# Key sums of the first attention from unsplit exponentials, and its values scaled one head later

## What is computed

```
scores = einsum('bhqd,bhkd->bhqk', q, k) / sqrt(128)
probs  = softmax(scores, axis=-1)
values = einsum('bhqk,bhkd->bhkd', probs, v)     # = v * probs.sum(over q)
out    = einsum('bsf,fh->bsh', values, w_o)
```

## Time and profile before

| | |
|---|---|
| median of 3 runs | 847.89 us |
| profiled execution | 848.14 us |
| its span, first to last instruction | 846.3 us |
| TensorE busy | 782.1 us, 92% |
| VectorE, ScalarE, GpSimd busy | 64%, 43%, 44% |
| granted TensorE clock, mean | 0.969 of 2.4 GHz |
| heads of the first attention | about 17 to 241 us |

### The profile page before, as it was taken

How to read it: one execution, slowest core, us unless ns; L and a number is a source line. 1 busy time by engine, 2 the same in 40 slices (tenths; PEclk the granted TensorE clock), 3 DMA queues, 4 the chain that set the end, 5 groups by cost and what they waited for, 6 DMA issues and landing times. The chain is left out here.

```text
span 846.3 us, 12715 instructions
## 1 busy us (share of the span) xinstructions
PE 782.1 (92%) x4092; PEld 599.9 (71%) x4092; DVE 538.5 (64%) x1049; ACT 359.8 (43%) x843; POOL 373.7 (44%) x339
## 2 busy tenths in 40 slices
PE   7899999999969889999999997988887896999997
PEld 5788888888844457888888885754445343788886
DVE  4666666677678964333333357799984698864535
ACT  3555555555541062232323234368884001543422
POOL 2221212123118924656565643799972885521100
PEclk9999999999989979999999999999999897999999
DMA  9210101010201014433333340000000012000001
GB/s 317 65 51 25 50 25 50 25 50 27 68 13 43 20 58 112 131 112 107 112 107 116 90 121 10 1 2 1 2 2 1 25 50 69 0 16 17 1 1 50
DMA packets 27054, 45.24 MB, mean 53 GB/s; under 512 B 3424, under 2 KB 16608, under 8 KB 26752
## 3 DMA queue, kind: packets, MB, share of 16 engines
q1 hardware_dynamic: 27008, 44.65, 17.7%
HBM read 43.45 MB, written 1.18 MB: 53 GB/s over the span
## 5 line engine op out<-in xcount | busy, mean ns | idle before, releaser
L1479 PE MATMUL bank<-xTh,ringh 128*128 128x512 f32 x420 | 169.5, 403 | 0.6 <-DVE xTl L1150 0.6
L1480 PE MATMUL bank<-xTl,ringh 128*128 128x512 f32 x420 | 166.2, 396 | 0.0
L1481 PE MATMUL bank<-xTh,ringl 128*128 128x512 f32 x420 | 166.0, 395 | 0.0
L1219 DVE TENSOR_TENSOR arena<-bank,arena 128x512 f32<-128x512 f32 x48 | 33.2, 691 | 114.9 <-ACT arena L881 105.7
L1481 PEld LDWEIGHTS bank<-xTh,ringl 128*128 128x128 f32 x420 | 79.3, 189 | 18.9
L1479 PEld LDWEIGHTS bank<-xTh,ringh 128*128 128x128 f32 x420 | 79.6, 190 | 16.7 <-issue 1.6
L1480 PEld LDWEIGHTS bank<-xTl,ringh 128*128 128x128 f32 x420 | 79.5, 189 | 15.1
L632 POOL TENSOR_TENSOR arena<-arena 128x512 f32<-128x512 f32 x48 | 62.6, 1303 | 51.6 <-DVE HTl L1223 49.5
L881 ACT ACTIVATE arena<-bank 128x512 f32<-128x512 f32 x48 | 28.7, 598 | 126.1 <-PE bank L1481 126.0
L555 POOL CAST ringh<-ring 128x768 fp32r<-128x768 f32 x15 | 12.7, 846 | 152.4 <-DMA ring<-w_attn 149.4
L1517 PE MATMUL bank<-outh,HTh 128*128 128x256 f32 x192 | 54.9, 286 | 3.1 <-DVE outl L1064 1.2
(11 more groups left out here) (269 smaller groups left out, 1971.7 us busy)
## 6 DMA issues: line engine op xcount, KB each, us to landing
ring<-w_moe SPq DMA_DIRECT2D x24, 256.0 KB, 2.9
arena<-route SPq DMA_DIRECT2D x16, 384.0 KB, 4.1
ring<-w_attn SPq DMA_DIRECT2D x15, 384.0 KB, 3.2
toep<-toep SPq DMA_DIRECT2D x32, 128.0 KB, 2.1
arena<-route SPq DMA_DIRECT2D x16, 256.0 KB, 4.1
outring<-w_down SPq DMA_DIRECT2D x24, 128.0 KB, 2.1
outring<-wo_attn SPq DMA_DIRECT2D x16, 128.0 KB, 2.0
arena<-route SPq DMA_DIRECT2D x16, 128.0 KB, 4.0
```

The costliest lines, as they stand in the source:

```text
L1219: dve.tensor_tensor(H1[:, i % LAG, :], bank[:, 1 + i % 2, :], SG[:, i % 2, :], ALU.mult).then_inc(gu_done, 1)
L1479: pe.matmul(o, ringh[:, slot, wc], xTh[:, k, halves[j]], start=(k == 0), stop=False)
L1480: pe.matmul(o, ringh[:, slot, wc], xTl[:, k, halves[j]], start=False, stop=False)
L1481: ins = pe.matmul(o, ringl[:, slot, wc], xTh[:, k, halves[j]], start=False, stop=(k == DK - 1))
```

## The change

For heads 0 to 14 the key sums are made another way. The exponentials E stay as they are, undivided and unsplit. VectorE writes the inverse row sums 32 times side by side (`inverse`), and TensorE multiplies, for each batch, these 32 columns (stationary) with E (moving, 128 columns) as one fp32 product into 32 rows of bank 2: eight products, the four batches of a half in four column groups (`sum_keys`). ScalarE copies the 256 columns out (`evac_key_sums`). SP writes one row of each group, 4 KB in all, to a buffer in DRAM, waits for it, and reads it back broadcast to all 128 rows (512 KB); it issues the next output weights and the next ring after that. `scale_v` then reads the sums from SBUF. Scaling and splitting of head h-1 move into head h on VectorE and ScalarE: on VectorE the two `scale_v` stand between the two row maxima and the two `low_v` behind the second, on ScalarE the two `high_v` stand between the two groups of exponentials, behind the copy of the first queries. TensorE's output product stays where it was; the key sums stand before chunks 2 to 5. Head 15 keeps the former way; its VectorE work and output weights come after the scaling and splitting of head 14. A semaphore that nothing used is dropped.

```diff
@@ -238,6 +238,10 @@
         VT = take(2 * TOK).rearrange("p (s t) -> p s t", s=2)
         VTc = take(TOK)
         E = take(TOK)
+        key_sums = take(2 * 2 * S).rearrange("p (s n) -> p s n", s=2)
+        spread_sums = take(2 * TOK).rearrange("p (s t) -> p s t", s=2)
+        inverse = take(B * 32).rearrange("p (b c) -> p b c", b=B)
+        sums_out = nc.dram_tensor("sums_out", (2, TOK), F32, kind="Internal").ap()
         outh = sb("outh", [P, 2, D], F32R)
         outl = sb("outl", [P, 2, D], F32R)
         nmax = sb("nmax", [P, B])
@@ -451,10 +457,26 @@
             load_x(1)
             sp.dma_start(outring[:, 0, :], wo_attn0[0, :, :]).then_inc(outring_in[0], 16)
 
+            def spread_key_sums(h, slot):
+                sp.wait_ge(ks_evac, h + 1)
+                settle(sp, sp_settled)
+                if not isinstance(h, int) or h >= 2:
+                    sp.wait_ge(sums_moved[slot], 16 * (h - slot))
+                    settle(sp, sp_settled)
+                    sp.wait_ge(vc_done, 2 * (h - 1))
+                    settle(sp, sp_settled)
+                sp.dma_start(sums_out[slot, :].rearrange("(j g s) -> g j s", j=2, g=4),
+                             key_sums[::32, slot, :].rearrange("g (j s) -> g j s", j=2)).then_inc(sums_moved[slot], 16)
+                sp.wait_ge(sums_moved[slot], 16 * (h - slot) + 16)
+                settle(sp, sp_settled)
+                sp.dma_start(spread_sums[:, slot, :], sums_out[slot, :].partition_broadcast(P)).then_inc(sums_moved[slot], 16)
+
             def load_attn0(h, slot):
                 sp.wait_ge(w_split, count(h - 1))
                 settle(sp, sp_settled)
                 sp.dma_start(ring[:, slot, 0:A_WO], w_attn0[h, :, :]).then_inc(ring_in[slot], 16)
+                if not isinstance(h, int) or h >= 2:
+                    spread_key_sums(h - 2, slot)
                 sp.wait_ge(wo_split, count(h - 1))
                 settle(sp, sp_settled)
                 sp.dma_start(outring[:, slot, :], wo_attn0[h, :, :]).then_inc(outring_in[slot], 16)
@@ -472,7 +494,9 @@
                 for w in range(2):
                     sp.dma_start(lowB[RANK * e:RANK * (e + 1), :, w, :], rows[w, e, :, :, :]).then_inc(lowb_in, 16)
             sp.dma_start(bias_bc[:], bias1.partition_broadcast(P)).then_inc(bias1_in, 16)
-            with sp.Fori(1, NH // 2) as i:
+            load_attn0(2, 0)
+            load_attn0(3, 1)
+            with sp.Fori(2, NH // 2) as i:
                 load_attn0(2 * i, 0)
                 load_attn0(2 * i + 1, 1)
 
@@ -506,6 +530,7 @@
 
             for h in range(4):
                 load_toep(toep0, 0, h, h)
+            spread_key_sums(NH - 2, 0)
             for n in range(2):
                 load_moe(n)
                 load_down(n)
@@ -785,15 +810,14 @@
 
             def exps(h, j):
                 act.wait_ge(nmax_done, 2 * h + j + 1)
-                act.wait_ge(el_done, count(2 * (h - 1) + j + 1))
+                act.wait_ge(ks_done, count(h))
                 for b in range(4 * j, 4 * j + 4):
                     ins = act.activation(E[:, b * S:(b + 1) * S], bank[:, 2 + j, (b % 4) * S:(b % 4 + 1) * S], ACT.Exp,
                                          bias=nmax[:, b:b + 1], scale=DH ** -0.5, accum_out=rowsum[:, b:b + 1])
                 ins.then_inc(exp_done, 1)
 
             def high_e(h, j):
-                act.wait_ge(en_done, 2 * h + j + 1)
-                act.wait_ge(csum_done, count(2 * (h - 1) + j + 1))
+                act.wait_ge(en_done, j + 1)
                 half = slice(j * HALF, (j + 1) * HALF)
                 act.activation(Eh[:, half], E[:, half], ACT.Copy).then_inc(eh_done, 1)
 
@@ -809,25 +833,33 @@
                 act.wait_ge(used, at)
                 act.activation(outh[:, slot, :], outring[:, slot, :], ACT.Copy).then_inc(wo_hi, 1)
 
+            def evac_key_sums(h, slot):
+                act.wait_ge(ks_done, h + 1)
+                if not isinstance(h, int) or h >= 2:
+                    act.wait_ge(sums_moved[slot], 16 * (h - slot))
+                act.activation(key_sums[:, slot, :], bank[:, 2, 0:2 * S], ACT.Copy).then_inc(ks_evac, 1)
+
             def head(h, slot):
                 last = isinstance(h, int) and h == NH - 1
+                exps(h, 0)
                 if not last:
                     evac_q(h + 1, 1 - slot, 0)
-                else:
+                if not isinstance(h, int) or h > 0:
+                    high_v(h - 1, 0)
+                    high_v(h - 1, 1)
+                exps(h, 1)
+                if last:
                     high_out(h, slot, out0_done, count(h - 1))
-                exps(h, 0)
-                if not last:
-                    evac_q(h + 1, 1 - slot, 1)
-                exps(h, 1)
-                high_e(h, 0)
-                high_e(h, 1)
-                if not last:
-                    high_out(h, slot, out0_done, count(h - 1))
-                high_v(h, 0)
-                high_v(h, 1)
-                if not last:
-                    evac_v(h + 1, 1 - slot, 0)
-                    evac_v(h + 1, 1 - slot, 1)
+                    high_e(h, 0)
+                    high_e(h, 1)
+                    high_v(h, 0)
+                    high_v(h, 1)
+                    return
+                evac_q(h + 1, 1 - slot, 1)
+                evac_key_sums(h, slot)
+                high_out(h, slot, out0_done, count(h - 1))
+                evac_v(h + 1, 1 - slot, 0)
+                evac_v(h + 1, 1 - slot, 1)
 
             for j in range(2):
                 evac_q(0, 0, j)
@@ -1039,6 +1071,11 @@
                 dve.tensor_scalar(nmax[:, 4 * j:4 * j + 4], mx[:, 4 * j:4 * j + 4], -(DH ** -0.5), None, ALU.mult)\
                     .then_inc(nmax_done, 1)
 
+            def invert(h, j):
+                dve.wait_ge(exp_done, 2 * h + j + 1)
+                dve.reciprocal(inverse[:, 4 * j:4 * j + 4, :], rowsum[:, 4 * j:4 * j + 4].unsqueeze(2).broadcast_to([P, 4, 32]))\
+                    .then_inc(rinv_done, 1)
+
             def recip(h, j):
                 dve.wait_ge(exp_done, 2 * h + j + 1)
                 dve.reciprocal(rinv[:, 4 * j:4 * j + 4], rowsum[:, 4 * j:4 * j + 4]).then_inc(rinv_done, 1)
@@ -1048,7 +1085,7 @@
                     .then_inc(en_done, 1)
 
             def low_e(h, j):
-                dve.wait_ge(eh_done, 2 * h + j + 1)
+                dve.wait_ge(eh_done, j + 1)
                 half = slice(j * HALF, (j + 1) * HALF)
                 dve.tensor_tensor(El[:, half], E[:, half], Eh[:, half].bitcast(F32), ALU.subtract)\
                     .then_inc(el_done, 1)
@@ -1065,32 +1102,44 @@
                     .then_inc(wo_split, 1)
 
             def scale_v(h, slot, j):
-                dve.wait_ge(csum_done, 2 * h + j + 1)
+                half = slice(j * HALF, (j + 1) * HALF)
+                if isinstance(h, int) and h == NH - 1:
+                    dve.wait_ge(csum_done, j + 1)
+                    sums = bank[:, 2 + j, :]
+                else:
+                    dve.wait_ge(sums_moved[slot], 16 * (h - slot) + 32)
+                    sums = spread_sums[:, slot, half]
                 dve.wait_ge(act_evac, 4 * h + 3 + j)
                 dve.wait_ge(vl_done, count(2 * (h - 1) + j + 1))
-                dve.tensor_tensor(VTc[:, j * HALF:(j + 1) * HALF], bank[:, 2 + j, :],
-                                  VT[:, slot, j * HALF:(j + 1) * HALF], ALU.mult).then_inc(vc_done, 1)
+                dve.tensor_tensor(VTc[:, half], sums, VT[:, slot, half], ALU.mult).then_inc(vc_done, 1)
 
             def head(h, slot):
                 last = isinstance(h, int) and h == NH - 1
+                first = isinstance(h, int) and h == 0
                 row_max(h, 0)
+                if not first:
+                    scale_v(h - 1, 1 - slot, 0)
+                    scale_v(h - 1, 1 - slot, 1)
                 row_max(h, 1)
+                if not first:
+                    low_v(h - 1, 0)
+                    low_v(h - 1, 1)
                 if last:
                     low_out(h, slot)
-                recip(h, 0)
-                recip(h, 1)
-                low_e(h, 0)
-                if not last:
-                    evac_k(h + 1, 1 - slot, 0)
-                low_e(h, 1)
-                if not last:
-                    low_out(h, slot)
-                scale_v(h, slot, 0)
-                if not last:
-                    evac_k(h + 1, 1 - slot, 1)
-                low_v(h, 0)
-                scale_v(h, slot, 1)
-                low_v(h, 1)
+                    recip(h, 0)
+                    recip(h, 1)
+                    low_e(h, 0)
+                    low_e(h, 1)
+                    scale_v(h, slot, 0)
+                    low_v(h, 0)
+                    scale_v(h, slot, 1)
+                    low_v(h, 1)
+                    return
+                invert(h, 0)
+                invert(h, 1)
+                evac_k(h + 1, 1 - slot, 0)
+                low_out(h, slot)
+                evac_k(h + 1, 1 - slot, 1)
 
```

(33 more changed lines are left out.)

## The result

The changed kernel takes 879.77 us (median of 4 runs, 877.70 to 881.35) against 846.84 of the kernel before on the same chips: a ratio of 1.0381, 95% interval 1.0357 to 1.0404. It is slower by 33 us; 885 was forecast. The profiled execution took 880.93 against 848.14, so +32.8 where the sum said +36.9.

A forecast was written before the change was run, and what follows sets the result against it. TensorE bounds the loop, busy 179.74 of 180 us. Waits +28.6 and +0.7, key sums -3.4, head 0 -2.7, head 15 +3.3, clock +10.4: +36.9 on 848.14, so 885 us, range 853 to 897.

The forecast's parts named there:

- The new wait: Before each head's output product, TensorE waits 0.7 us for the low part of the values, without any collision.
- The collision: GpSimd's subtraction on the ring holds up VectorE's low part; TensorE waits 2.2 us instead of 0.7 in heads 1 to 13.
- the ring's landing: Next ring of weights, queued behind the 512 KB broadcast, lands 9.4 us after key sums start; GpSimd starts 0.2 later.
- rival 1: No collision: the ring lands 1.3 us later or GpSimd gets in early, so only the chain counts; 855 us, chance 0.2.
- Head 14 at 0.7 of wait: Head 14 has no ring left to split, so TensorE's wait before the output product is only 0.7 us.
- The clock: Half of the 13 heads get a 1.2 GHz stretch after their wait, 1.6 us each: +10.4 us, bounds 0 and +20.8.
- Key sums: Eight fp32 products, column groups side by side, take 0.70 us instead of 0.94: a gain of 0.24 a head.
- Rival 4: Key-sum column groups run one after another: 1.1 us more in 15 heads, +16 on the forecast, 901 us, chance 0.04.
- The transfers: Key sums go through DRAM and land 1.5 us into the next head, half a microsecond before VectorE wants them.
- The ends: First and last heads of the loop: head 0 gains 2.7 us, head 15 loses 3.3 us.
- The wait of 1.45: In head 0 TensorE waits 1.45 us before the key sums, short of the wait that lowered the clock.
- two reciprocals 0.4: In head 0's chain to the key sums, VectorE's two reciprocals of the row sums together take 0.4 us.

The follow-up runs named there:

- e1: Changed kernel plus one wait on GpSimd: it splits the ring of head h+2 only after both low parts of head h-1 are out; 860.96 us, ratio 1.0169.
- e3: e1 with TensorE's output product of head h-1 also moved one projection chunk later; 846.70 us, ratio 0.9990 to the kernel before.
- e4: Changed kernel, both transfers kept, but in heads 0 to 14 scaling multiplies the values with themselves, not waiting for the sums; 882.47 us, ratio 1.0409.
- e7: Changed kernel with inverse row sums made as four reciprocals and a spreading copy, not one reciprocal of 128 columns; 879.33 us, ratio 1.0384.
- e6: e3 with the eight key-sum products issued twice over, same result; 853.46 us, ratio 1.0082 to the kernel before.
- e5: e3 with last-head orders changed: next convolution product before head 14's output product, high part of output weights before exponentials; 843.82 us, ratio 0.9961.

## Why the prediction was right, step by step

**The new wait: right.** The chain from the first scores to the output product was put at 5.28 us, 0.72 beyond the cover; in e1, without the collision, it is 139.87 - 134.56 = 5.31. The low part started 4.56 after the first scores, 4.6 in the prediction. In the period the chain stands at 0.88 (e1 less e3), 0.16 more: the first product after a wait takes 0.22 us up to the next one, where 0.12 is usual, and the rest isn't located.

**The collision: right in kind, a little too large, and by the forecast instruction in four heads of 13.** I had 2.2 us for both, measured are 0.88 + 1.09 = 1.97. The step that was off is the ring's landing: "the ring lands at T + 9.4". With T = 139.61 it was issued at 144.49, T + 4.9, and GpSimd began on it at 148.49, T + 8.9, against T + 9.6 forecast: 4.0 us from issue to use where the kernel before took 3.3 (169.09 to 172.43), so 0.7 for the queue ahead of it, not the 1.2 in my sum. So GpSimd began at 2.6 of the head instead of 3.4, before the second scaling was through. It caught that scaling and the scaled copy of the maximum, and the low part was late because it stands behind that copy in VectorE's order. I had listed an earlier phase as a collision too, but had priced only what starts inside GpSimd's pass, not what queues behind it. Nor does the phase stand still, as I had it ("it hangs on T alone"): over the 13 heads GpSimd began at 1.4 to 3.2. In heads 4, 6, 11 and 13 it began after the second scaling had started (2.8 to 3.2), its conversion was the one held up (1.19 to 1.32 us, 0.89 in head 13), the subtraction then ran from 4.15 to 6.0, and the low part was stretched as forecast; the output product came at 6.63 to 6.66, 6.75 in the prediction. In heads 1 and 2, below the start of 2 down to which I had counted, the wait was there too (1.87 and 2.28), so the half of rival 1 that let GpSimd in early falls; the other half, a ring 1.3 us later, didn't come about.

**Head 14 at 0.7 of wait:** idle 0.66 in the trace, period 14.72, that of the loop in e1. Right.

**The clock: a quarter, not half.** 13 waits of 1.68 to 2.28 us were followed by 3 stretches of low clock, not 6.5, each worth 17.45 - 15.77 = 1.7 us or a little over: +5.4 instead of +10.4. The size of one was right. What I had wrong is how many waits are that long. Over the changed kernel, e4 and e7, 39 waits of this kind in all, none of the 18 of 1.58 to 1.74 us was followed by low clock, and 10 of the 21 of 1.81 to 2.29 us were: about the half that I had counted, but only six of the 13 waits of the changed kernel were in that group. These are three executions; over the four of the changed kernel the mean granted clock went from 0.962 (881.35 us) to 0.970 (877.70 us), so the number of stretches isn't fixed.

**Key sums: the sign right, the gain half.** 0.83 a head for 0.70. The columns were 0.45, by e6; what I had put at 0.12 for the way in and 0.13 for the way out (0.58 less 0.45) is 0.38 in all. Rival 4, the groups one after another, falls by the same run. The Trainium skill's sentence that a weight load overlaps running products only when its row group differs (TensorE: Matmul & The Clock Gate, Part 3) doesn't hold for these column groups: 16 more loads with their 16 products took 0.45 us. Its other one, that a change of tiling mode drains the array (TensorEngine Tiling, Key Properties), is what the 0.38 looks like, though no run separates a drain from the other costs of switching.

**The transfers: right.** The first transfer was issued at 156.92 and the second at 158.65, T + 1.6 and T + 3.3 from the key sums at 155.37, against T + 1.8 and T + 3.8 forecast. No row stood behind the 0.65 us for SP in that sum; from the end of the copy (156.54) to the first issue it was 0.38. In e3, where the sums arrive later in the head, VectorE waited for them:

```profile
138.34 0.33 SPq L472 DMA_DIRECT2D arena<-sums_out  x1
...
142.62 1.29 DVE L1118 TENSOR_TENSOR arena<-arena 128x512 f32<-128x512 f32 x2 [0.72 <-DMA arena<-sums_out]
```

That is 4.3 us from issue to use. At that rate the sums landed in the changed kernel 1.3 us into the head, against 1.5 forecast and 2.0 needed, and e4 agrees that nothing waited for them.

**The ends: both missed, in opposite terms of one sum.** Head 0 gained 0.43 instead of 2.7. The wait of 1.45 was 2.12, and behind it the clock fell, where I had counted that gain as sure. The term that was mis-sized is "two reciprocals 0.4":

```profile
22.62 0.95 DVE L1076 RECIPROCAL arena<-rowsum 128x128 f32<-128x128 f32 x1 [0.72 <-ACT arena L815]
...
23.63 0.69 PE L1573 MATMUL bank<-arena 128*32 128x128 f32 x16 [2.12 <-DVE arena L1076]
```

The first of the two is over while ScalarE still makes the second group of exponentials, so one alone is in the chain, and it takes 0.95: 0.55 of the 0.67 that was missing. In e7 a narrow one and a copy stand in its place, the wait is 1.61 and the clock stays in that execution. The last head lost 4.70 instead of 3.3. A wait of 2.96 was there (3.2 forecast), and the first reciprocal of its softmax came at 6.6 (6.9 forecast), 3.1 later than before. What wasn't in the sum is the stretch of low clock from 263.0: in it the output product took 266.44 - 262.00 = 4.44 us for 2.87, and the key sums of head 15 stand behind it and the convolution product. The second stretch, from 273.3, cost nothing up to the transposes, which came 6.06 us after VectorE's first addition of the norm (273.67), 6.07 before. e3 and e5 show that order alone takes most of it back.

Sum of the steps as measured: 13 x 1.09 = 14.2 for the collision; 14 x (0.88 - 0.11) = 10.8 for chain and key sums; 5.4 for the clock; together 30.4, against 30.28 in the table; with the ends and the rest 32.8. That the total came so near is in part luck, since its misses went both ways: the forecast had the waits 2.8 us, the clock 5.0 and the rest of the kernel 1.7 too dear, and the key sums 1.9, head 0 2.3 and head 15 1.4 too cheap. Why the rest of the kernel came out 1.7 us shorter wasn't looked into.

## What to carry to other kernels

Where one engine is full, work taken off the others is worth nothing, but a result that must now arrive inside a fixed stretch of the full engine has a chain to price: write down its start, each step in the order that each engine executes, and the moment that it is asked for. Then look at what the new transfers move in time on engines that hold each other up: here a ring of weights that GpSimd took up some 1.5 us later in a head cost more than the chain (1.09 against 0.88 us a head). And what stands behind a held instruction is held too; place the consumer's order first, as e1 and e3 did by one wait and one moved call, before judging the new way by its first total.

## What the runs showed of the hardware beyond what was expected

A reciprocal of 128 columns takes 918 ns on VectorE where one of 4 columns takes 171 and a copy of 128 columns 270: between these two widths the reciprocal costs about 6 ns a column. Eight fp32 products in four column groups cost 0.45 us more when doubled: 13 of 14 periods of e6 are 14.25 or 14.26 us, 11 of 14 of e3 13.80 or 13.81. GpSimd's subtraction (1.83 alone) and VectorE's operations on SBUF stretched each other in either order: 2.15 to 2.24 on one side, 1.07 for 0.17, 2.01 for 0.69 and 2.33 for 0.69 on the other, never the PSUM reduction between them (0.68 to 0.69 in all 32). In these heads the one that had started first ran on and the other stood. And waits of the same length were not followed by the same clock: of two of 1.91 us in the changed kernel (before 199.84 and 231.57) only the second was.
